# Routing of a block one step sooner in phase one of an RWKV and mixture-of-experts kernel

## The reference

```python
x = x + rwkv(layernorm(x))                 # r, k, v, g projections; att = r@k masked by decay; state carried on
h = layernorm(x)
probs = softmax(h @ gate_w.T)              # 8 experts, the two largest per token
count = cumsum(one_hot(top2))              # per batch: place of the token in its expert's queue
keep  = count <= capacity                  # 320 rows per expert and batch
x = x + sum_e probs_e * w2_e(silu(w1_e h) * w3_e h)   # for the kept (token, expert) pairs
```

## Time and profile before

| | us |
|---|---|
| median of 3 runs (lowest, highest) | 846.95 (845.86, 848.41) |
| the profiled execution | 846.3 |
| its span, from first to last instruction | 844.6 |
| PE busy in the span | 814.7 |
| DVE busy | 505.7 |
| ACT busy | 464.4 |
| POOL busy | 468.3 |

### The profile page before, as it was taken

The page is one execution under the profiler, slowest core; times in us unless marked ns, Lnnn a source line. Parts: engine busy times, 40 slices in busy tenths (PEclk is TensorE's granted clock), DMA queues, the critical chain, the costliest instruction groups (busy, mean ns, idle before and its releaser), DMA issues. The chain is left out here.

```text
span 844.6 us, 17509 instructions
## 1 busy us (share of the span) xinstructions
PE 814.7 (96%) x6291; PEld 674.5 (80%) x6291; DVE 505.7 (60%) x1286; ACT 464.4 (55%) x860; POOL 468.3 (55%) x529
## 2 busy tenths in 40 slices
PE   5999999999999989899999999999999999999997
PEld 4777787777777667678998788898788899788886
DVE  6789988899998886343543543544443545353441
ACT  4478877778787667264543543644552544453331
POOL 6445577777777857475444356453436452535215
PEclk9999999999999999999999999999999999999999
DMA  5852032213111121546333334342415442413114
GB/s 163 334 209 70 28 108 68 76 52 96 40 40 48 58 91 72 178 157 135 101 70 40 110 95 70 95 113 27 124 60 79 121 106 26 95 35 44 20 14 50
DMA packets 50746, 74.30 MB, mean 88 GB/s; under 512 B 5072, under 2 KB 42448, under 8 KB 50640
## 3 DMA queue, kind: packets, MB, share of 16 engines
q1 hardware_dynamic: 35760, 53.72, 19.2%
q0 software_dynamic: 14592, 19.18, 13.6%
q10 hardware_dynamic: 288, 0.01, 0.0%
HBM read 38.67 MB, written 34.22 MB: 86 GB/s over the span
## 5 line engine op out<-in xcount | busy, mean ns | idle before, releaser
L1648 POOL DMA_INDIRECT out<-ysb,index x80 | 124.7, 1558 | 145.6 <-DVE ysb L1887 111.1
L2001 PE MATMUL p<-xh,whi 128*128 128x512 f32 (+2 forms) x504 | 185.4, 368 | 1.4 <-POOL wlo L1637 0.5
L1863 DVE TENSOR_TENSOR hid<-gated,p 128x512 f32<-128x512 f32 (+1 forms) x126 | 81.0, 643 | 176.2 <-ACT gated L1710 176.2
L2003 PE MATMUL p<-xh,wlo 128*128 128x512 f32 (+2 forms) x504 | 185.3, 368 | 0.0
L2002 PE MATMUL p<-xl,whi 128*128 128x512 f32 (+2 forms) x504 | 184.6, 366 | 0.0
L2027 PE MATMUL py<-w,hh 128*128 128x512 f32 x448 | 162.5, 403 | 4.2 <-DVE hl L1132 3.7
L1710 ACT ACTIVATE gated<-p 128x512 f32<-128x512 f32 (+1 forms) x126 | 70.8, 562 | 157.4 <-PE p L2003 152.8
L1637 POOL TENSOR_TENSOR wlo<-wraw,whi 128x448 fp32r<-128x448 f32 x56 | 70.8, 1267 | 89.8 <-ACT whi L1696 84.4
L2001 PEld LDWEIGHTS p<-xh,whi 128*128 128x128 f32 x504 | 94.7, 188 | 19.2 <-issue 3.5
L2026 PE MATMUL py<-w,hl 128*128 128x256 f32 x384 | 108.5, 283 | 0.0
L2002 PEld LDWEIGHTS p<-xl,whi 128*128 128x128 f32 x504 | 94.8, 188 | 15.2
(11 more groups left out here) (215 smaller groups left out, 1430.7 us busy)
## 6 DMA issues: line engine op xcount, KB each, us to landing
wraw<-in_w SPq DMA_DIRECT2D x24, 896.0 KB
disp<-wraw SPq DMA_DIRECT2D x16, 662.5 KB, 8.2
xtok<-disp SPq DMA_DIRECT2D x16, 530.0 KB, 4.8
x_ring<-in_x SPq DMA_DIRECT2D x16, 256.0 KB, 3.3
out<-x SPq DMA_DIRECT2D x16, 256.0 KB
xtok<-disp SPq DMA_DIRECT2D x8, 265.0 KB
out<-ysb,index POOLq DMA_INDIRECT x80
disp<-row,slot_i POOLq DMA_INDIRECT x64
```

What stands on the lines that cost most here:

```text
L1648: nc.gpsimd.indirect_dma_start(out, bass.IndirectOffsetOnAxis(ap=index[e.const % 2][:, t:t + 1], axis=0), ysb[j % NY][:], None, compute_op ...
L1863: nc.vector.tensor_tensor(hid[k][:, 0:w], gated[k][:, 0:w], p3[k][:, 0:w], ALU.mult).then_inc(hid_ready, 1)
L2001: nc.tensor.matmul(dst[:, 0:w], hi[m][:, wcut], xh[xcut], start=(kt == 0), stop=False)
L2003: ins = nc.tensor.matmul(dst[:, 0:w], lo[m][:, wcut], xh[xcut], start=False, stop=(kt == KT - 1))
```

## The change

Only orders and waits change; each instruction of before is there once, but that the last `gated` runs on DVE instead of POOL.

- DVE, in each step: `best_two(c - 2)` and `tally(c - 2)` go from behind `decayed_k` to ahead of `residual`; `slots` takes block c - 2 instead of c - 3 and stands behind `decayed_k`, with `logit_max` and `stats2`; `stats1(c + 3)` goes behind these from step 0 on.
- PE: `count` takes block c - 2 instead of c - 3 and stands behind `project_o(c - 1)` instead of ahead of it. The waits on masks and slots are adapted.
- POOL: `scatter` takes block c - 3 instead of c - 4 in each step; before, the lag was caught up by two scatters in step 13. Step 14 now has two. `weight_low` and, on ACT, `weight_high` go one step sooner, and the third weight's load on SP too.
- Tails: `count(12)`, `slots(12)`, `scatter(12)` and one weight piece are gone from them, `gated(15)` is on DVE, `slots(14)` stands ahead of the first low parts, and ACT's `logit_exp(15)` goes ahead of `early_gate(3)`.

```diff
@@ SP
-            if b in (1, 3, 8):
+            if b in (1, 3, 7):
@@ POOL, step c
             gated(c - 1)
-            if c < TAIL - 1:
-                scatter(c - 4, range(0, 1))
+            scatter(c - 3, range(0, 1))
             decayed_r(c + 1)
...
-            if c < TAIL - 1:
-                scatter(c - 4, range(1, TPS))
-            weight_low(c - 6)
-            if c >= TAIL - 2:
-                scatter(c - 3)
+            scatter(c - 3, range(1, TPS))
+            weight_low(c - 5)
+            if c == TAIL - 1:
+                scatter(c - 2)
             norm1(c + 3)
@@ POOL, tail
         weight_low(10)
-        weight_low(9)
-        scatter(12)
-        chain.reset()
+        weight_low(11)
         norm2(14)
-        gated(15)
         scatter(13)
...
         norm2(15)
-        weight_low(11)
         scatter(14)
@@ ACT, step c
-            weight_high(c - 4)
+            weight_high(c - 3)
@@ ACT, tail
         early_gate(2)
-        weight_high(11)
         early_hidden_hi(2)
+        logit_exp(15)
         early_gate(3)
+        normed2(15)
         early_hidden_hi(3)
-        logit_exp(15)
         early_gate(4)
-        normed2(15)
@@ DVE, the new function
+        def gated_last(b):
+            dve.wait_ge(z_ready, b + 1)
+            dve.wait_ge(gT_ready, b + 1)
+            wait(dve, wo_done, b)
+            nc.vector.tensor_tensor(zg[:], z[:], gT[b % 2][:], ALU.mult).then_inc(zg_ready, 1)
@@ DVE, step c
             state_b(c)
-            stats1(c + 3)
...
             mixing(c + 1, 2)
+            best_two(c - 2)
+            tally(c - 2)
+            if c < 0:
+                stats1(c + 3)
...
             residual(c - 1)
             logit_sum(c - 1)
-            slots(c - 3)
-            logit_max(c - 1)
-            stats2(c - 1)
...
             decayed_k(c + 1)
...
-            best_two(c - 2)
-            tally(c - 2)
+            slots(c - 2)
+            logit_max(c - 1)
+            stats2(c - 1)
+            if c >= 0:
+                stats1(c + 3)
             mask(c + 1, 0, 0)
@@ DVE, tail
         tally(13)
-        slots(12)
-        chain.reset()
         residual(14)
...
         normed_y(15)
+        gated_last(15)
...
         stats2(15)
+        slots(14)
         chain.reset()
...
         early_hidden(2)
-        slots(14)
-        chain.reset()
@@ PE, scores_a(b) and count(b)
-                wait(pe, slot_ready, b - 3)
+                wait(pe, slot_ready, b - 2)
...
-                pe.wait_ge(attm_ready[HGS - 1], min(TPS * b + 8, TPS * STEPS))
+                pe.wait_ge(attm_ready[HGS - 1], min(TPS * b + 6, TPS * STEPS))
@@ PE, step c
-            count(c - 3)
             project_o(c - 1)
+            count(c - 2)
             logits(c + 1)
@@ PE, tail
-        count(12)
         within(15, 1, 3)
         project_o(14)
...
+        count(13)
         group_sums(15)
-        count(13)
...
         project_o(15)
+        count(14)
         early_up(2)
-        count(14)
```

More of the change, by code:

```diff
@@ L497, in on_sync @@
                 load_x(b + RING)
-            if b in (1, 3, 8):
-                first_weights((1, 3, 8).index(b))
+            if b in (1, 3, 7):
+                first_weights((1, 3, 7).index(b))
             if b == EARLY_B + 2:
@@ L1146, in on_vector @@
             state_b(c)
-            stats1(c + 3)
+            mixing(c + 1, 2)
+            best_two(c - 2)
+            tally(c - 2)
+            if c < 0:
+                stats1(c + 3)
             if c == -3:
                 center_gate()
-            mixing(c + 1, 2)
             if c == -1:
```

## The result

The changed kernel takes 854.0 us (median of six executions, 851.8 to 856.8) against 846.35 for the kernel before on the same chip: 1.0093 times as long, with a 95% interval from 1.0072 to 1.0114. The forecast was 847.0 with a range up to 851.5, so it was too low by 7 us; it had given a slower kernel a chance of 0.18. The profiled execution has a span of 853.3 us, against 844.6.

What follows compares the result with a forecast made beforehand. PE's time goes straight into the end, and a ring of PE and DVE through count sets phase one's steady step. Terms +1.6 + 1.1 - 2.1 - 0.5 = +0.1 us on 846.95 gave 847.0 us, range 841.5 to 851.5.

Steps and rivals of the forecast that it cites:

- the step of block 2 to 3: Phase one, ahead of the eleven steps: it now holds the first count, and turn_k starts at 74.07, not 72.42; +1.6 us.
- the eleven steps: Phase one, turn_k of block 3 to that of block 14: 18.5 us each instead of 18.40; +1.1 us in all.
- the catch-up: Phase one's last interval, block 14 to 15, where a second scatter delayed norm2: 21.32 becomes 19.2 us; -2.1 us.
- all behind it: The tail, behind turn_k of block 15: net -0.5 us, bounds -2.0 and +0.5.
- the ring of counts: Steady step of phase one: PE from count to masked_kv, 9.09 us, then DVE to tally's end, 9.44; together 18.53 us.
- The first full step with a count: The step of block 2 to 3: decayed_r may hold mixing, so tally ends later and turn_k starts at 74.07; +1.6 us.
- The tail: End of phase one: early slices start 1.5 us sooner, but logit_exp(15) delays a gate; net -0.5 us.
- The wait for `hid`: Tail, early slices: PE idles about 1.8 us at slice 5, since logit_exp(15) makes the gate of slice 3 late.
- The 3.69 us at the seam: PE's wait for the last low part, between phase one and phase two: forecast to stay.
- The second rival: Steady steps: POOL's decayed_r holds tally, some 1.2 us longer a step; 852 for four such steps, 860 for eleven; chance 0.17.
- The first rival: Steady steps come near PE's own time, 18.15 us each: 842.5 us in all, 841.2 at the 18.04 floor; chance 0.30.

Runs made afterwards that it cites:

- e12: e1 with GpSimd's decayed_r moved between the third and fourth scatter transfers of the step; 852.3 us.
- e1: The changed kernel with GpSimd's norm2 of block c-1 at the end of step c, ahead of norm1, instead of in step c+1; 883.3 us.
- e13: e1 with best_two and tally ahead of mixing(2) on VectorE, and decayed_r between the third and fourth scatter transfers on GpSimd; 844.8 us.
- e15: e13 with the last logit_exp and normed2 back where the kernel before has them, and weight_low between norm2 and norm1; 837.3 us.
- e10: e1 with best_two and tally ahead of mixing(2) on VectorE, and decayed_r behind all four scatter transfers on GpSimd; 862.5 us.

## Why the prediction was wrong

Term by term, forecast and then measured in the profiled executions: the step of block 2 to 3 +1.6 and +1.9 us, the eleven steps +1.1 and +8.0, the catch-up -2.1 and -1.9, all behind it -0.5 and +0.8; the sum +0.1 and +8.7.

**The step that failed** is the term of the eleven steady steps, +1.1 us, which measured +8.0. It takes the ring of counts for the only one. That ring was sized well: e12 has it at 18.47 to 18.55 us. But in the changed kernel it makes two steps at most, and the sign of it that the forecast named, TensorE waiting 0.5 us at `count`, is in none of the eleven. Eight of them are made by another ring: GpSimd's `norm2`, then ScalarE's exponential, gate and z, then GpSimd's gating, scatter, `decayed_r`, `weight_low` and `norm1` again, with TensorE's `project_k` waiting for the gate beside it. Five steps of 19.56 hold 5 x 1.06 = 5.3 us of the 6.9 by which the eleven exceed 11 x 18.5; the step of 19.90 below holds 1.4 more.

The forecast had one way into this ring in hand. It said that `norm1` waits for `stats1`, "which now ends just ahead of the masks", and used that only as a reason why GpSimd would not be *earlier* for the tally. It did not ask who stands behind `norm1`. With `stats1` back at its old place (e3) the gate comes in time again, which speaks for `stats1` as what makes GpSimd late in the first place, but e3's steps are longer for another reason, so this start of it is not shown. Nor did the forecast turn the lock round: it priced a VectorE operation held by GpSimd, but not GpSimd's four tiny operations held by VectorE's `diff` and `mixed`. `nbias`, 0.20 us, became 1.04.

**The first full step with a count** behind it was foreseen (`turn_k` forecast at 74.07, measured at 74.28). What followed was not: the clock at its lower level for 3.6 us in the step behind, which took 19.90 us, 1.4 over 18.5. The forecast treated waits of TensorE as costing their own length only, though the earlier trace rows had a lowered clock behind a wait.

**The catch-up** was right: 19.39 us against 19.2, with `decayed_r` on the tally as said. Its `took` was held for 1.22 us there, and TensorE waited 1.21 us for the count.

**The tail** was to give 0.5 us, and from `turn_k` of block 15 to the end 0.8 us were lost. Up to the first matmul of phase two it did gain, 0.9 us (46.5 us instead of 47.4), although much was spent on the way. The wait for `hid` was forecast at 1.8 us and is 1.95; that the clock falls behind it was missed, the same omission as above: from 340.84 to 343.83 matmuls follow each other at 0.43 us instead of 0.23, some 1.4 us in all. The 3.69 us at the seam of the earlier trace rows are 3.05 now. `project_o(15)` comes 22.4 us behind `turn_k` of block 15 instead of 25.3, so the sooner start was real, and most of it was spent on these. Phase two then takes 1.7 us longer than before. Half of that stands ahead of its first `turn`, where TensorE waits 1.29 us for the rows of the queue instead of 0.42:

```profile
350.58 0.61 PE L2026 MATMUL py<-w,hh 128*128 128x512 f32 x1 [3.05 <-DVE hl L1131]
...
358.59 1.09 PE L1982 MATMUL pt<-ident,xtok 128*128 128x128 f32 x8 [1.29 <-DMA xtok<-disp]
```

The other half was not followed up.

**The second rival** had the right mechanism, and its range of 852 to 860 holds the result. But its margin of 0.3 us was too small: in e1 the last addition is held although it starts 0.5 to 0.65 us ahead of `decayed_r`. So was its price of 1.2 us: a step of e1 with a meeting takes 20.2 to 20.3 us at full clock, 1.8 over 18.5, and 22.7 where the clock falls. And in the changed kernel it is not what makes the time: in the steady steps it is the late gate that keeps `decayed_r` away from `tally`. It is the case of a right range for another reason.

**The first rival**, steps near TensorE's own time, was wrong for the changed kernel, but e13 shows that it needs only three moves of other engines' work. Its floor of 18.04 us was 0.17 too high for the new order, in which eight steps of e13 take 17.9.

By the SBUF - State Buffer page of the Trainium skill (Who interferes with whom), VectorE and GpSimd exclude each other through a shared port pair, in either direction, and casts and `tensor_scalar` operations can take the pair too. The rows agree: `nbias` was held by `mixed`, `before` by `r_dec`, and, with one input only, `took` and `slot_i` by `wlo`.

## What to carry to other kernels

When an operation moves on one engine, list every ring that passes through it, not only the one it is taken out of: follow the wait that it ends on the other engine, and what is queued behind that wait. Where VectorE and GpSimd share a port, a schedule is right only as a pair: put large GpSimd operations beside VectorE's masks, which take one operand from PSUM, as e15 does, and not back to back. Operations on a single operand are not safe, as `took` and `slot_i` show. Count a tiny operation on the critical way at least as long as the large one it may meet. A repair that removes one wait can bring two operations together that the wait had kept apart, so look at durations, not at waits alone.

## What the runs showed of the hardware

- A VectorE operation of 0.17 us takes 0.6 to 2.0 us when it meets one GpSimd operation of 1.15 to 1.3 us, and 2.73 when it meets two that follow each other. In these rows it is held although its record begins 0.3 to 0.7 us ahead of the record of the GpSimd operation (191.08 against 191.72, 202.06 against 202.76). In these cases GpSimd was still issuing a scatter transfer when the VectorE operation began. In e10 one that began at 188.16 us, in a transfer that another transfer followed, took its 0.17. Why the later one wins was not tested.
- In the other direction GpSimd's operations on two columns go from 0.23 to 0.72 and from 0.20 to 1.04 us beside VectorE's `diff` and `mixed`, which have two inputs.
- A single wait of TensorE of 1.15 us, ahead of short matmuls, was followed 1.4 us later by 3.6 us at 1.2 GHz, and one of 1.95 us, 1.1 us later, by about 3 us. Waits of 1.45 us ahead of `project_k` were not followed by any, in five steps. Nor were one of 1.21 us at `count` in the last step of the changed kernel (clock 1.00 from 302 to 336 us) and the one of 2.14 us of e1 shown above. What tells the cases apart stays open.
